# Embedding of a two-layer token model: row choice and gathers batch by batch, mask memsets behind them, four identity products ahead of the first transposes

## What is computed

```
# ids x: (4, 512); base_weight: (50257, 192); train_weight: (256, 192); tune_ids: 256 vocabulary ids
id2row = jnp.full((VOCAB,), -1).at[tune_ids].set(jnp.arange(NUM_TUNE))
out = base_weight[input_ids]
rows = id2row[input_ids]
h = jnp.where((rows >= 0)[..., None], train_weight[jnp.maximum(rows, 0)], out)
h = h + attention(layernorm(h), Wq, Wkv, Wproj)      # 12 heads of 16, first key masked for all but the first query
h = h + moe_ffn(layernorm(h), ...)
h = h + ttt_attention(layernorm(h), ...)
h = h + soft_moe(layernorm(h), phi, scale, ...)      # phi is normalised over its 192 rows, times scale
```

## Time and profile before

| | us |
|---|---|
| median of 3 timed runs | 1375.83 |
| the runs | 1373.02, 1375.83, 1375.84 |
| the profiled execution | 1372.88 |
| its span, first to last instruction | 1371.1 |
| TensorE busy in the span | 1252.3 (91%) |
| VectorE, ScalarE, POOL busy | 912.3, 729.3, 381.5 |
| mean granted clock of TensorE, as a share of full speed | 0.963 |

### The profile page before, as it was taken

How to read it: one execution, slowest core, us unless ns; L and a number is a source line. 1 busy time by engine, 2 the same in 40 slices (tenths; PEclk the granted TensorE clock), 3 DMA queues, 4 the chain that set the end, 5 groups by cost and what they waited for, 6 DMA issues and landing times. The chain is left out here.

```text
span 1371.1 us, 29272 instructions
## 1 busy us (share of the span) xinstructions
PE 1252.3 (91%) x11347; PEld 862.8 (63%) x11347; DVE 912.3 (67%) x2294; ACT 729.3 (53%) x1529; POOL 381.5 (28%) x445
## 2 busy tenths in 40 slices
PE   4889999799779999899999998899986899899998
PEld 3532333345647777677777776777864445588888
DVE  6588888413578777799888877888874899400001
ACT  1446555432224443688888884788874334443310
POOL 6500000100057777456666660000000344200000
PEclk9889999979989999999999999999998999999999
DMA  3342121300024234634343452122102300177811
GB/s 99 106 124 70 47 61 34 72 15 1 21 74 124 82 117 128 204 111 124 109 132 98 140 137 64 41 64 59 47 1 93 129 1 1 39 274 276 281 69 46
DMA packets 99287, 127.42 MB, mean 93 GB/s; under 512 B 24590, under 2 KB 87805, under 8 KB 94957
## 3 DMA queue, kind: packets, MB, share of 16 engines
q1 hardware_dynamic: 96556, 123.44, 29.5%
q0 software_dynamic: 1536, 1.59, 0.5%
q10 hardware_dynamic: 1056, 0.52, 0.1%
HBM read 89.06 MB, written 37.88 MB: 93 GB/s over the span
## 5 line engine op out<-in xcount | busy, mean ns | idle before, releaser
L1792 POOL TENSOR_SCALAR r_grD<-gr 32x192 f32<-32x192 f32 x192 | 101.8, 530 | 93.8 <-DVE gr L1686 45.9
L700 ACT ACTIVATE PT<-bank 128x1024 f32<-128x1024 f32 x96 | 94.3, 1023 | 59.5 <-PE bank L580 58.8
L641 DVE TENSOR_REDUCE mx<-bank 128x1 f32<-128x512 f32 x176 | 110.0, 682 | 12.2 <-PE bank L563 11.9
L1523 PE MATMUL bank<-r_grD,ek 128*128 128x256 f32 x384 | 100.0, 396 | 0.0
L2554 DVE TENSOR_TENSOR eo_all<-bank,m_b2s 128x768 f32<-128x768 f32 x8 | 7.7, 958 | 138.5 <-PE bank L2515 138.5
L2546 ACT ACTIVATE x_g<-bank,m_b1s 128x128 f32<-128x128 f32 x192 | 51.4, 399 | 75.7 <-PE bank L2497 75.7
L1523 PEld LDWEIGHTS bank<-r_grD,ek 128*128 128x128 f32 x384 | 67.7, 189 | 9.3
L2428 POOL TENSOR_SCALAR m_xs<-m_xs 128x256 f32<-128x256 f32 x4 | 2.5, 632 | 247.6 <-DVE m_xs L2319 247.6
L1736 ACT ACTIVATE r_t<-r_xh,r_cd 128x64 f32<-128x64 f32 x192 | 70.2, 429 | 0.8
L1514 PEld LDWEIGHTS bank<-gr,r_A 128*128 128x128 f32 x384 | 47.6, 190 | 33.7 <-DVE gr L1686 32.6
L1352 POOL TENSOR_TENSOR rope_c<-cy,p_rope 128x512 f32<-128x512 f32 x48 | 60.0, 1270 | 20.0 <-DVE cy L1205 20.0
(11 more groups left out here) (380 smaller groups left out, 3235.3 us busy)
## 6 DMA issues: line engine op xcount, KB each, us to landing
wb<-in_m_w SPq DMA_DIRECT2D x32, 1152.0 KB, 5.6
ek<-k_d SPq DMA_DIRECT2D x32, 384.0 KB
k_d<-t_late SPq DMA_DIRECT2D x46, 256.0 KB, 2.8
tgt<-c_d SPq DMA_DIRECT2D x33, 196.0 KB
c_d<-t_late SPq DMA_DIRECT2D x32, 196.0 KB, 2.9
g_d<-gr SPq DMA_DIRECT2D x32, 192.0 KB
o_G<-g_d SPq DMA_DIRECT2D x32, 192.0 KB, 3.0
qk_d<-a_parts SPq DMA_DIRECT2D x24, 192.0 KB, 3.0
```

The lines of the kernel that those rows point to most:

```text
L641: v.tensor_reduce(mx[u % 2][:, j // 4, j % 4:j % 4 + 1], slot(f"A{u}.{j}"), AX.X, ALU.max).then_inc(*dve.did(f"max{u}.{j}"))
L700: a.activation(PT[kt % 2][:, 2 * hp:2 * hp + 2, :], STB[s % 2][:, :, :], ACT.Exp, scale=DH ** -0.5)\
L1523: last = t_.matmul(SP_[g][:, i * B * E1:(i + 1) * B * E1], ek[r][:, p, :], grD[g][:, i, :, :].rearrange("p b e -> p (b e)"), start=False, ...
L1792: last = g_.tensor_scalar(grD[g][rr, :, b, :], b3(gr[j % RING][rr, cols(g)]), 0.0, None, ALU.bypass)
```

## The change

1. The id load and the load of the tuned ids get semaphores of their own (`ids_in`, `tune_in`); VectorE converts the ids after the first alone, and waits for the second only ahead of the comparisons. The integer copy of the ids now stands in front of the float copy.
2. The row choice becomes a function `tuned_rows(b)` for four tiles, with its four steps for each batch. It runs for batch 0, batch 1, then the mask memsets, then batch 2; batch 3 comes behind `layer_norm(0)` and the scaling of phi. POOL's `train(b)` waits for `tuned.b`.
3. POOL's part of the masks stands behind the overrides of batch 0; on SP the copies of the mask rows stand behind the stores of phi.
4. `layer_norm(0)` stands in front of the scaling of phi (`scaled_slots`). TensorE waits for the scaled phi (`normed`) ahead of the q/k products, whose banks it frees, and no more ahead of the transposes.
5. Four identity products (`fill`) stand behind the products that spread `unit`, ahead of batch 0's transposes.

```
-                sp.dma_start(ids16[:, :], ...).then_inc(loaded, 16)
+                sp.dma_start(ids16[:, :], ...).then_inc(ids_in, 16)
...
+                for k in range(KC):
+                    sp.wait_ge(normed, k + 1)
+                    sp.dma_start(M["phin_d"][k * DC:(k + 1) * DC, :], phi[:, k, :]).then_inc(phi_out, 16)
                 sp.wait_ge(cleared, 2)
                 for r in C[1:]:
...
-                for k in range(KC):
-                    sp.wait_ge(normed, k + 1)
-                    sp.dma_start(M["phin_d"][k * DC:(k + 1) * DC, :], phi[:, k, :]).then_inc(phi_out, 16)
...
                 last.then_inc(spread, 1)
+                fill(t_, VB[1], ident, 4)
...
                     t_.wait_ge(*dve.at(f"xn.{b}"))
-                    if b == 0:
-                        t_.wait_ge(normed, 2)
...
                     t_.wait_ge(*act.at(f"xT1.{b}"))
+                    if b == 0:
+                        t_.wait_ge(normed, 2)
...
-                v.memset(Q[0][MASK_ROW:MASK_ROW + 1, :, :], NEG)
-                v.memset(K[0][MASK_ROW:MAX_ROW + 2, :, :], 1.0).then_inc(cleared, 1)
-                v.wait_ge(loaded, 32)
+                v.wait_ge(ids_in, 16)
...
+                def tuned_rows(b):
+                    of = slice(b * TB, (b + 1) * TB)
+                    for t in range(b * TB, (b + 1) * TB):
+                        last = v.scalar_tensor_tensor(hit[:, t, :], tune_f[:, :], ids_f[:, t:t + 1], rank_f[:, :],
+                                                      ALU.is_equal, ALU.mult)
...
+                    v.tensor_reduce(best[:, of], hit[:, of, :], AX.X, ALU.max).then_inc(*dve.did(f"best.{b}"))
...
+                tuned_rows(0)
+                tuned_rows(1)
+                v.memset(Q[0][MASK_ROW:MASK_ROW + 1, :, :], NEG)
+                v.memset(K[0][MASK_ROW:MAX_ROW + 2, :, :], 1.0).then_inc(cleared, 1)
+                tuned_rows(2)
...
                 layer_norm(0)
+                scaled_slots()
+                tuned_rows(3)
...
-                g.wait_ge(cleared, 1)
-                g.memset(Q[0][MASK_ROW:MASK_ROW + 1, :, 0:1], 0.0)
-                g.memset(K[0][MASK_ROW:MASK_ROW + 1, :, 1:N], 0.0).then_inc(cleared, 1)
...
-                    g.wait_ge(*dve.at("tuned"))
+                    g.wait_ge(*dve.at(f"tuned.{b}"))
...
                     train(b)
+                    if b == 0:
+                        g.wait_ge(cleared, 1)
+                        g.memset(Q[0][MASK_ROW:MASK_ROW + 1, :, 0:1], 0.0)
+                        g.memset(K[0][MASK_ROW:MASK_ROW + 1, :, 1:N], 0.0).then_inc(cleared, 1)
```

More of the change, by code:

```diff
@@ L104, in embed @@
         firsts = lambda after: [f"A{j}" for j in range(*AT_PE[after])]
-        dve = Steps(sem("e_dve"), ["eps", "idsf", "ids", "rank", "hits", "best", "none", "tuned"]
-                    + [f"{n}.0" for n in ("stats", "aggr", "rstd", "xn")]
+        dve = Steps(sem("e_dve"), ["eps", "idsf", "ids", "rank"] + [f"{n}.{b}" for b in range(3) for n in ("hits", "best", "none", "tuned")]
+                    + [f"{n}.0" for n in ("stats", "aggr", "rstd", "xn")] + [f"{n}.3" for n in ("hits", "best", "none", "tuned")]
                     + [s for b in SB for s in (peaks(0, 3) if b + 1 == B else []) + [f"rest0.{b}"] + (peaks(3, 5) if b + 1 == B else []) + [f"rest1.{b}"]
@@ L244, in _, with scaled_slots @@
                 v.tensor_scalar(unit[:, :], unit[:, :], scale[:, 0:1], None, ALU.mult).then_inc(united, 1)
-                v.wait_ge(spread, 1)
-                for k in range(KC):
-                    for hf in range(2):
-                        cols = slice(hf * SL // 2, (hf + 1) * SL // 2)
-                        last = v.tensor_tensor(phi[:, k, cols], phi[:, k, cols], QK[hf][0:DC, :], ALU.mult)
-                    last.then_inc(normed, 1)
+                def scaled_slots():
+                    v.wait_ge(spread, 1)
+                    for k in range(KC):
+                        for hf in range(2):
+                            cols = slice(hf * SL // 2, (hf + 1) * SL // 2)
+                            last = v.tensor_tensor(phi[:, k, cols], phi[:, k, cols], QK[hf][0:DC, :], ALU.mult)
+                        last.then_inc(normed, 1)
                 def layer_norm(b):
```

32 lines of the change are left out of this document (15 added, 17 removed).

## The result

| | before | changed |
|---|---|---|
| median of 20 runs each, us | 1377.67 | 1372.14 |
| lowest and highest | 1370.76, 1381.02 | 1364.04, 1374.82 |
| the profiled execution, and its span | 1372.88, 1371.1 | 1364.04, 1362.2 |
| mean granted clock | 0.963 | 0.967 |

The ratio is 0.9961, with a 95% interval of 0.9945 to 0.9976: faster by 5.5 us between the medians (3.3 to 7.6 by the interval), which is 0.4%. The changed kernel was measured twice more, beside other kernels, with ratios of 0.9953 (0.994 to 0.9967) and 0.9968 (0.9947 to 0.9988). The profiled execution of the changed kernel is the fastest of its 20, so its span flatters the change: 8.9 us less, where the medians give 5.5. The kernel before has runs anywhere from 1370.76 to 1381.02 us, not two levels as its first three seemed to show.

The account below looks back on a forecast made before the run. It took TensorE's late first transposes in `embed` and its slow clock behind them as the bound. Gains of 1.96, 2.75 and 0.9 made 5.6 us; 1369.0 us lay between 1367.3 and 1370.2, range 1365.2 to 1373.5.

Parts of the forecast that it names:

- Ids earlier: VectorE's id conversion waits for the ids load alone: 4.2 us earlier, first base gather from 8.39 to about 4.2.
- Row choice and memsets: VectorE's queue: four pieces of 3.1 us and 3.5 us of memsets put size at 20.0 to 20.4, 0.4 us lost.
- Identity products: TensorE ahead of batch 0's transposes: 3.6 us of pure delay, bought back only by the clock; transposes at 28.5.
- Batch 0 at full clock: TensorE's interval from batch 0's to batch 1's transposes: 10.64 us instead of 13.39, 2.75 gained.
- Batch 1: TensorE's interval from batch 1's to batch 2's transposes: 12.7 us with the 2.38 us gap kept, 0.9 gained.
- Batch 2: TensorE's interval from batch 2's to batch 3's transposes: unchanged, 10.64 us before.
- First score 2.6 behind the fourth transposes: First score product on TensorE, waiting for Q and K rows, moves along with the fourth transposes, some 2.6 us behind.
- The level: Starting time: profiled run less 5.6 gives 1367.3 us, median of three less 5.6 gives 1370.2; 1369.0 taken between.
- Fill slow: Identity products run slow or don't lift batch 0's clock: net gain 1.4 to 2.4 us, 1371 to 1374.5; chance 0.10.
- Gather queue: POOL's gathers become the bound, batch 3's rows up to 2 us late: gain 3.5, 1370 to 1372.5; chance 0.12.
- Held gathers: Comparison runs on VectorE hold POOL's gathers, 9.7 us in all: batch 3's transposes 2.8 us later, 1378.6; chance 0.05.
- Gain doesn't get through: Clock drops at the block's end or in later stages give back some 3.4 us: 1372 to 1376; chance 0.11.

Follow-up runs that it names:

- pair of controls: Changed kernel and kernel before, each run again untouched: changed 1371.08 us against 1376.24, ratio 0.9953; kernel before 1378.45 us in a single execution.
- last version: Changed kernel with slot norms before batch 2's row choice, batch 3's piece and mask work later: 1369.1 us without identity products, 1369.02 with them.
- second trace without identity products: Rerun, in the third group, of the changed kernel with only its four identity products taken out: 1369.64 us, ratio 0.9958.
- first four kernels: Changed kernel without identity products 1379.48 us; kernel before plus them 1380.03; changed kernel with slot norms first, with them 1379.56, without 1378.3; beside 1380.81.

## Why the prediction was right, and where it wasn't

The forecast was a gain of 5.6 us at the fourth transposes. The trace has 5.68 there, and the medians 5.5. That the two agree to 0.1 us is luck. The mechanism, the clock of batch 0 kept up by bringing its transposes close behind the spread, is right; but the terms were off by -0.5 (the start of batch 0), +0.3 (batch 0), +2.0 (batch 1) and -1.7 (batch 2), and they cancelled. In the pair of controls the gain at the fourth transposes is 4.45 us, made of 0.35, 4.16, -0.05 and -0.01.

- **Ids earlier: 4.2 forecast, 5.65 measured.** The conversion of the ids took 1.67 us instead of 0.74. It ran beside POOL's memset L375 (1.39 to 3.93), and ended at 4.00, just behind it; before it had run at 6.66, when that memset was over. The gather then began 0.95 us after the last copy of the ids. It cost nothing: the last override of batch 0 stood at 17.59, where 17.0 was forecast and 19.8 would have done (the statistics began at 22.00, and 2.16 is the time from issue to use of the earlier trace rows).
- **Row choice and memsets: size forecast at 20.0 to 20.4, measured at 21.40.** Comparisons from 7.15 as forecast (7.2). A piece takes 3.25 and not 3.1: the reduction of 1024 elements is 1.22 us, where a quarter of 4.42 is 1.11. The two memsets take 4.4 us with their gaps (0.48 and 0.37), where the sum had 3.5 to 3.9. From 7.15 to 21.40 is 14.25, where 3 x 3.1 + 3.5 made 12.8: 0.5 of the difference lies in the pieces and 0.9 in the memsets. So the spread came at 22.14 and not 20.9: 1.7 us lost on this chain, where the sum had 0.4. On the path to batch 0's transposes this is the term that was mis-sized most, and the last version takes it out (size at 18.91, right behind the root).
- **Identity products: 3.6 forecast, 3.60 measured**, and 4.00 to 4.59 in later traces that have them behind the spread, within the bounds. T0 came at 29.04, or 30.08 and 30.02 in the later traces, against 28.5. So of the 1.96 us that were to be gained here 1.42 were, and 0.35 in the pair of controls. The reading "pure delay, bought back only by the clock" was half right: delay, yes, but the clock had come up without them. With the statistics brought forward the transposes follow the spread at once. The prediction took the rise at 24.3 from the window of the earlier trace rows, where the clock reads 1.00; but it reads 1.00 from 0 to 20 us too, while the products run at the slow rate, so that window doesn't show a rise. What shows it is the rate of the products that follow the spread: 0.45 us each with the fill on the kernel before (23.96), and still 0.24 for the transposes at 25.68 without it.
- **Batch 0 at full clock: 2.75 forecast, 3.02 measured** (interval 10.37), and 4.16 in the pair of controls (14.33 to 10.17).
- **Batch 1: 0.9 forecast, 2.94 measured.** The sum kept the gap of 2.38 us of the earlier trace rows, since nothing in the change touches it. Nothing did: the second trace of the kernel before hasn't got it either. A gap of one execution was read as one of the kernel, and 0.9 was the middle between two outcomes that the changed kernel had neither of.
- **Batch 2: unchanged forecast, 1.70 lost.** The clock fell in the ordinary gap of 1.15 us. In the other two traces of the changed kernel it held there.
- **First score 2.6 behind the fourth transposes:** measured 1.27, 2.78 and 3.16. It is short where batch 2 ran slow (also 1.38 in the second trace without identity products), probably since the stores and loads had more time.
- **The level.** I took 1369.0, between the profiled execution and the median of three runs, less 5.6. The median of 20 is 1372.14, inside the range. The three runs of before had a median of 1375.83, those 20 of 1377.67: 1.8 of the 3.1 us were in my starting point, and most of the rest in the step below the median, taken for a lower level that 20 runs don't show.

The rivals. *Fill slow* (1): partly, up to 4.57 instead of 3.60 in the traces of the changed kernel, and in none of them with a slow batch 0. *Gather queue* (2): not in the changed kernel; the last override is issued at 53.67, and the statistics of batch 3 at 58.94 didn't wait. The forecast's 52.6 to 57.5 for its landed rows can't be redone from the terms given: 13.1, 5.2, 2.0 and three times 10.5 make 51.8, and 59.2 with a wait of 2.45 in each batch, and batch 3 has six gathers, not eight. But it is the next bound: it appears at once without the pieces, and in the two traces without identity products that have no long wait of ScalarE. *Held gathers* (3): none of the four pieces of comparisons held one for longer than 0.3 us in the changed kernel (0.95 to 1.22 beside them); the subtractions did (40.04, 2.59 us; at 50.71 one took 1.35). The Trainium skill (GPSIMD Engine Reference, section 1, Specifications) says that POOL contends with VectorE instructions of two SBUF inputs. The trace agrees where a gather was held, and most gathers beside such instructions weren't. *Gain doesn't get through* (4): no; the stages behind the block moved by 0.4 to 1.6 us in the one pair of traces, to both sides, and the medians have 5.5.

## What to carry to other kernels

Bring what is queued for a batch into the order in which the batches need it, and ask of every step in such a queue which batch it serves: pieces of the row choice and the statistics' place were each needed for the gain here, since without either one the times were those of the kernel before. Before adding products to keep TensorE's clock up, ask whether the work already there, moved together, does it: here the order closed the idle time of 6.25 us, and the products put in between only moved the transposes back. And a gap or a clock drop of one profiled execution is no term of a sum until a second execution has it.

## What the hardware showed that I hadn't expected

- **The clock falls in small gaps, sometimes.** The same idle time of 1.14 to 1.15 us ahead of q/k products was followed by 1.2 GHz for about 3.4 us in three traces (batch 2 of the changed kernel, batch 1 with phi scaled first, batch 2 in the second trace without identity products, which has another idle time of 1.70 us ahead of its transposes), at a price of 1.7 us each, and by nothing in the twenty other places that have it. What decides it stays open.
- **ScalarE held for 4 to 6 us by a "remote" releaser** in the traces of three of the first four kernels (and 1.75 us in the fourth), ahead of copies out of the banks of batch 1, and in none of the eight that came later, four of them on the same chip. It cost up to 11 us of idle TensorE. Its cause is open.
- **A long gather ends a fixed distance behind VectorE's run.** Most gathers take 0.94 to 1.28 us, beside VectorE's comparisons and subtractions too. But all 16 that took 1.86 us or more, over the fourteen traces, ended 0.82 to 0.89 us behind the end of the run of two-input instructions that they started in: the long run ended at 14.96 and the gather at 15.78; in one piece 13.39 and 14.21; with phi scaled first (one piece of four) 33.26 and 34.09; the three subtractions 46.20 and 47.09, 41.76 and 42.63 in the changed kernel. So a gather held in this way costs what is left of the run, and short runs cap the price. Seven more took 1.35 to 1.54 us beside subtractions and follow another pattern: five ended 0.27 to 0.28 us behind the run, two before its end. Which gathers are held isn't settled: beside subtractions from 35.08 one that started at 35.52 took 1.12, and beside those from 45.73 one at 46.15 took 2.35 (both in the last version without identity products).
- **The wait for batch 3's base rows varies between executions.** Ahead of its overrides POOL stood 4.25 us in the first trace of the changed kernel, 3.53 and 3.56 in the later two, and 2.46 in the kernel before. SP's stores of q/k parts were under way in all of them, so they alone don't explain it. There was room for it.
